# A macaron transformer block in which TensorE chooses between two programs: which of the two stands first behind the branch

## What is computed

```python
x = x + 0.5 * ffn(layernorm(x))
x = x + attn(layernorm(x))
x = x + 0.5 * ffn(layernorm(x))
# ffn: g = (xf @ gate_w.T) * gate_s;  u = (xf @ up_w.T) * up_s
#      out = (silu(g) * u) @ down_w.T * down_s;   256 -> 704 -> 256
```

## Time and profile before

| what | value |
|---|---|
| median of 3 runs | 795.83 us (795.64 to 796.29) |
| the profiled execution, device time | 797.67 us |
| its span, first to last instruction | 795.7 us |
| TensorE matmuls busy | 774.0 us, 97% |
| DVE, ACT, POOL busy | 614.1, 549.8, 390.2 us |
| TensorE instructions | 6160 matmuls, 6160 weight loads |
| mean granted TensorE clock | 0.998 of 2.4 GHz |
| DMA | 89.76 MB, of which 0.85 MB in 52 packets are TensorE's instructions |

### The profile page before, as it was taken

The page is one execution under the profiler, slowest core; times in us unless marked ns, Lnnn a source line. Parts: engine busy times, 40 slices in busy tenths (PEclk is TensorE's granted clock), DMA queues, the critical chain, the costliest instruction groups (busy, mean ns, idle before and its releaser), DMA issues.

```text
span 795.7 us, 17286 instructions
## 1 busy us (share of the span) xinstructions
PE 774.0 (97%) x6160; PEld 524.3 (66%) x6160; DVE 614.1 (77%) x1267; ACT 549.8 (69%) x1065; POOL 390.2 (49%) x430
## 2 busy tenths in 40 slices
PE   6999999999999999999999999999999999999997
PEld 5888888776555555665555565544555457898886
DVE  5767577799898998998998799979988925465543
ACT  4866765445867878767777866778877997466652
POOL 3888777536335643163282243531322256566554
PEclk9999999999999999999999999999999999999999
DMA  9801264204365585244574453643841210210001
GB/s 328 350 2 64 96 159 121 41 3 103 107 170 156 171 224 128 60 122 150 162 195 136 106 128 121 185 86 87 222 108 52 67 44 17 67 38 28 27 27 55
DMA packets 61089, 89.76 MB, mean 113 GB/s; under 512 B 19788, under 2 KB 24268, under 8 KB 60748
## 3 DMA queue, kind: packets, MB, share of 16 engines
q1 hardware_dynamic: 60860, 88.57, 39.0%
q10 hardware_dynamic: 144, 0.07, 0.0%
HBM read 45.52 MB, written 40.76 MB: 108 GB/s over the span
## 4 chain that ended last, share of the span: by engine, by line
PE 82%; DVE 9%; ACT 3%; issue 2%; POOL 2%; DMA 1%; SPq 0%; DVEq 0%; ACTq 0%
PE psum L1010 17%; PE psum L1119 16%; PE psum L978 12%; PE psum L1102 12%; PE psum L1039 11%; PE psum L1077 10%; DVE NP L1366 4%; PE psum L1087 3%; DVE SH L1366 2%; PE psum L996 2%; ACT PT L1231 1%; POOL HL_f L1426 1%; DMA RD<-wd 1%; PE psum L988 1%; ACT XN L1160 1%
## 5 line engine op out<-in xcount | busy, mean ns | idle before, releaser
L1231 ACT ACTIVATE PT<-psum 128x512 f32<-128x512 f32 (+2 forms) x640 | 309.8, 571 | 107.4 <-PE psum L1102 106.0
L1366 DVE TENSOR_REDUCE NP<-psum 128x1 f32<-128x512 f32 (+3 forms) x448 | 261.0, 643 | 23.5 <-PE psum L1087 14.1
L1483 POOL TENSOR_SCALAR_AFFINE_SELECT PT<-PT 128x512 f32<-128x512 f32 x128 | 80.6, 636 | 184.4 <-ACT PT L1231 182.2
L1119 PE MATMUL psum<-PT,V 128*32 128x512 f32 (+3 forms) x1536 | 145.2, 496 | 0.0
L1102 PE MATMUL psum<-Q,K 50*128 50x512 f32 (+2 forms) x768 | 141.5, 408 | 1.8 <-DVE XL L1271 0.7
L1077 PE MATMUL psum<-K,Q 48*128 48x512 f32 (+2 forms) x768 | 138.3, 387 | 5.1 <-ACT PT L1231 2.6
L1010 PE MATMUL psum<-XH,WG_f 128*128 128x512 f32 x352 | 141.5, 402 | 0.0
L1010 PE MATMUL psum<-XL,WG_f 128*128 128x512 f32 x352 | 138.2, 393 | 0.0
L1426 POOL TENSOR_TENSOR HL_f<-HF_f,HH_f 128x512 fp32r<-128x512 f32 x80 | 103.1, 1299 | 70.2 <-ACT HH_f L1192 70.0
L1366 DVE TENSOR_REDUCE SH<-psum 128x1 f32<-128x512 f32 (+3 forms) x192 | 103.4, 590 | 13.5 <-PE psum L1087 12.6
L1102 PEld LDWEIGHTS psum<-Q,K 50*128 50x128 f32 x768 | 67.2, 184 | 70.6 <-DVE NP L1366 24.1
(11 more groups left out here) (89 smaller groups left out, 1049.4 us busy)
## 6 DMA issues: line engine op xcount, KB each, us to landing
zd<-ZH SPq DMA_DIRECT2D x32, 512.0 KB, 3.8
Q<-zd SPq DMA_DIRECT2D x64, 192.0 KB, 3.8
K<-zd SPq DMA_DIRECT2D x64, 192.0 KB, 4.7
zd<-ZL SPq DMA_DIRECT2D x16, 512.0 KB, 4.6
od<-OS SPq DMA_DIRECT2D x32, 256.0 KB, 2.5
OC<-od SPq DMA_DIRECT2D x32, 128.0 KB, 2.8
SC<-rd_ SPq DMA_DIRECT2D x32, 128.0 KB, 2.9
X<-x SPq DMA_DIRECT2D x7, 512.0 KB, 11.8
```

Of the source, the lines that this page charges most:

```text
L1119: ins = tn.matmul(bank(*piece)[32 * h:32 * h + 32, skip:512], V[b % 2][:, col:col + 32], pt_view(gr, c2, j)[:, h, :], start=(j == 0), stop ...
L1231: sc.activation(dst, src, ACT.Exp, scale=0.25).then_inc(S["act_exp"], 1)
L1366: ve.tensor_reduce(out=acc, in_=src, axis=AX, op=ALU.max, negate=True).then_inc(S["dve_max"], 1)
L1483: gp_.affine_select(out=pt, in_=pt, compare_op=ALU.is_ge, fill=0.0, base=0, pattern=[[0, 4], [1, P]], channel_multiplier=-1).then_inc(S["p ...
```

## The change

The test is turned round, and with it the order in which the two programs are written:

```diff
@@ -1667,11 +1667,11 @@
             flag = nc.tensor.alloc_register("general")
             nc.tensor.reg_load(flag, FLAG[0:1, 0:1])
             before = dict(pe.met)
-            with nc.tensor.If_eq(flag, 0):
-                tensor_program(pe, todo[cut + 1:], False)
+            with nc.tensor.If_ne(flag, 0):
+                tensor_program(pe, todo[cut + 1:], True)
             pe.met = before
             with nc.tensor.Else():
-                tensor_program(pe, todo[cut + 1:], True)
+                tensor_program(pe, todo[cut + 1:], False)
```

## The result

The changed kernel takes 802.53 us (median of 4 runs, 801.86 to 802.80) against 795.74 (4 runs, 795.49 to 796.29) for the kernel before: 6.8 us slower. The recorded ratio is 1.0091, interval 1.0077 to 1.0105 (the two medians alone give 1.0085). I had forecast 798.6 with a range up to 801.5. The direction was right, the forecast size (2.8 us) less than half of what came.

The account below looks back on a forecast made before the run. TensorE's matmuls, busy 97% of the span, were taken to bound the kernel; +3.19 + 1.2 + 0.3 - 1.9 = +2.8 us on the median 795.83 gave 798.6 us, range 796.9 to 801.5.

Parts of the forecast that it names:

- The branch jumps: At TensorE's branch at 16.1: a jump of 3.28 us in place of 0.09, +3.19 us, all on the path.
- the fetch runs in traffic: At the branch, 16.3 to 20.0: full DMA engines lengthen the code fetch, +1.2 us, bounded by 0 and 5.1.
- The bound from above (5.1): Most that traffic could add at the branch: a 3 KB transfer's 6.9 us against 1.8 in calmer parts, 5.1 more.
- The next block: Behind the first 15 to 18 matmuls after the branch: a 1.1 us stall for the next code, +0.3 us net.
- The clock: After the empty array at 16.3 to about 20.7: possible fall to 1.2 GHz, losing 1.7 us, left at 0.
- The end: At the last output DMA: without the jump's code fetch it lands in 1.8 us, not 3.7, -1.9 us.
- Rival C: At the kernel's end: the end gives nothing, some engine's share is late anyway; +4.7, 800.5 us, chance 0.07.
- From the profiled execution to the median: Whole kernel: the profiled 797.67 stood 1.84 above the runs' median, so 800.5 profiled and 798.6 for the median.
- Rival A: Behind the branch: clock or next block cost in full, +3.7 to +5.7, 799.5 to 801.5 us, chance 0.24.
- Rival B: At the branch: traffic costs nothing and the next block is in time, +1.3, 797.1 us, chance 0.14.
- Rival D: At the branch at 16.1: target resident or asked for early, start costs about 0.1 us; 794.0 us, chance 0.03.

Follow-up runs that it names:

- e5_wide: Changed kernel with the 8 small matmuls before the branch made four times as wide (512 columns instead of 128): 800.77 us.
- e2_both_jumps: Changed kernel with a second general program behind the ternary one, so TensorE jumps at the branch and again at the end: 804.17 us.
- e4_quiet: Changed kernel with SP holding its third weight copy and all behind it until ACT's first gate, so few transfers run at the branch: 803.61 us.
- e7_hint_late: Changed kernel with a prefetch hint for the branch's target behind the first transposes (about 11 us): 795.22 us, ratio 0.9997 to the kernel before.
- e3_hint: Changed kernel with a prefetch hint for the branch's target ahead of TensorE's first matmul: 796.05 us, ratio 1.0005 to the kernel before.
- e6_end_hint: Kernel before (ternary program first) with a prefetch hint 142 instructions ahead of the jump at its end: 794.14 us, ratio 0.9984.
- the single program: Kernel before with only the ternary program behind the flag's load, no branch, general program or jump: 793.54 us, ratio 0.9972.

## Why the prediction was right and wrong

The reading of the two places was right: the same trace had both prices of a branch, and the nine late packets were indeed a code fetch in the output's way. The size failed in two terms, the traffic and the clock.

1. *The branch jumps, +3.19, and the fetch runs in traffic, +1.2.* Together 4.4; measured 5.96 - 0.09 = 5.87 (6.06 and 6.22 us for the branch in `e5_wide` and `e2_both_jumps`). The traffic does lengthen the fetch, as `e4_quiet` shows with 3.62 us, but the traffic's term was sized by the wrong row. It is 2.3 to 2.7 us, not 1.2, since the packet starts 3.4 us behind the branch rather than 0.9. I had taken the transfer of the identity, on a queue of its own, as the nearest; it took 3.3 us and was issued before the engines were full (1.03). The bound from above (5.1) held.

2. *The next block, +0.3.* The pause is real and of the forecast size (1.1 us forecast, 0.79 idle and about 1.0 in all in `e5_wide`), and comes behind 20 matmuls, not 15 to 18. In the changed kernel it is covered by the slow matmuls (0.43 us apart). Of the 0.79 us of slack at the wait for ACT that I counted on, the delay shrinks by 0.34 us only (9.18 us ahead of it, 8.84 behind).

3. *The clock, left at 0 in the sum.* This is the step that failed outright. I listed it as a case of 0.24 with 1.7 us, on the ground that nothing in the trace showed a pause of 4 us in mid-kernel, which is the lack of a row and not a reason for 0. The pause was longer than forecast (6.12 us against 4.4), all four of the changed kernel's runs have mean grants of 0.993 to 0.996, and in its place the fall took 2.8 us. Without it the kernel gains 1.8 us (`e5_wide`). The evidence lay in the earlier trace rows: the clock was down (0.54) behind 4.8 us almost without work. It was down in the changed kernel (0.50 over 22.6 to 28.8), in `e2_both_jumps` (0.50 over 20.85 to 27.6) and, with only 2.95 us idle, in `e4_quiet` (0.50 over 19.05 to 22.4). It did not need the work to come back, as I had supposed: in the changed kernel it fell 0.7 us before. My 2.4 and 1.2 GHz stand for grants of 1.00 and 0.50; at 0.50 the matmuls of 512 columns begin 0.427 us apart (23.24 to 28.36 in twelve steps), which is 1.2 columns a ns. How long a pause has to be is not shown: at 525.7 in the kernel before it fell with no idle stretch over 0.33 us in the 7 us ahead, and behind the 1.04 us of `e5_wide` and the 0.51 us of `e7_hint_late` it stayed at 1.00.

4. *The end, -1.9.* Right: the landings go from 3.7 to 1.8, and the median from 795.6 to 793.5 without the jump. Rival C, by which the end gives nothing, is out.

5. *From the profiled execution to the median.* I carried 1.84 us over as a constant. It was in the main the one clock fall at 525.7 to 529.2, an accident of that execution. This makes 800.5 the wrong figure for a profiled execution, but it leaves the forecast of the median as it is, since the +2.8 is a difference. It is why the profiled executions differ by 5.1 us and the medians by 6.8.

The range failed with the two terms together. Rival A added the clock to a traffic of 1.2 us and so ended at 801.5; traffic and clock at their measured size were in none of the cases. Its lower end was also too low: it takes off 0.79 us of slack that the sum had already used. And the range ends at 801.5, where A ends, although the text says that it leaves out the worst of A.

With measured terms, against a kernel before without that fall: +5.9 for the branch, +0.5 as it begins later (16.55 against 16.06, flag load and all), +2.8 for the clock in its place, -0.3 made up by 62 us, -2.0 at the end: +6.9 against 6.8. The +0.5 belongs to this execution (`e2_both_jumps`, without it, has a longer branch, 6.22 us). Rival B (traffic costs nothing) fell with 5.96. Rival D fell too: no code packet starts before 19.97, 3.4 us behind the branch, though the hint of `e3_hint` did just what D supposed, with 0.39 us for the branch. A compare-and-branch that goes straight on took 90 and 94 ns (the kernel before, `e6_end_hint`); the branches whose target had been asked for took 0.35 to 0.48 us (`e6_end_hint`, `e3_hint`, `e7_hint_late`), and those to code that was not there 3.28 to 6.22 us (the kernel before, `e4_quiet`, the changed kernel, `e5_wide`, `e2_both_jumps`).

## What to carry to other kernels

Let the path that is usually taken go straight on at the branch, above all where the engine has no queued work and the DMA engines are full (0.09 us against 5.96 here, with 6.12 us of an idle array); put the far jump where the engine ends anyway (3.28 us here, of which nobody waits). Then look at what its code fetch meets: a block of code on one DMA engine just before the last output is waited for cost about 2 us here (a landing of 3.7 us instead of 1.8), and a prefetch hint some 140 instructions ahead removed nearly all of it (median 794.14 against 793.54 for the single program). Cost a pause of TensorE together with the clock behind it (6.12 us idle, then a grant of 0.50 over 6.8 us, here), and look for such one-time events before a profiled execution is laid over a median.

## What the runs showed that I had not expected

Each far jump without a hint brought two code packets close together here, and at the end of the kernel before the first cost nothing and the second about 2 us. The block behind the target was fetched 3.9 us after the target's in quiet and 5.8 in traffic (19.97 and 25.73). TensorE stopped again behind 20 matmuls where the clock was full, 0.79 us in `e5_wide` and 0.80 us in `e7_hint_late`. That the target stands near the end of its block is an estimate: 20 matmuls and their weight loads are 40 instructions, against 12320 in 52 packets, about 237 a packet.

The prefetch hint was not free here. At the very start (`e3_hint`) the flag's load came 1.4 us later with it (16.2 against 14.8); behind the transposes, which start at 10.01 us (`e7_hint_late`), it came 0.2 us later only (15.0), but then the fetch was only just done in time: its packet starts at 13.6 and ends at 14.6, execution went on 1.4 to 1.6 us after a packet's end at the other jumps, and the branch is at 16.4.
